# Splitting the output maps of a perceiver prologue into halves by head and placing each half behind its own batch of maxima

## What is computed

```python
x = layer_norm(image_embeds, ln1_g, ln1_b)
l = layer_norm(latents, ln2_g, ln2_b)
q = l @ Wq
kv = concatenate([x, l], axis=1) @ Wkv
k, v = split(kv, 2, axis=-1)          # 16 heads of 64
w = softmax(einsum('bhqd,bhkd->bhqk', q * scale, k * scale))
out = einsum('bhqk,bhkd->bhqd', w, v) # heads side by side: [16, 64, 1024]
return out @ Wo                       # [16, 64, 128]
```

## Time and profile before

| what | value |
|---|---|
| median of 3 runs | 948.94 us |
| lowest and highest | 947.06 and 949.42 us |
| the profiled execution's own time | 947.89 us |
| its span, first to last instruction | 946.2 us |
| mean granted TensorE clock | 0.994 |
| PE busy | 909.3 us (96%) |
| DVE busy | 798.4 us (84%) |
| ACT busy | 701.2 us (74%) |
| POOL busy | 378.3 us (40%) |

### The profile page before, as it was taken

One profiled execution on the slowest core, in us unless ns is written; L12 is line 12 of the kernel. 1 busy time (PEld: TensorE's weight loads), 2 busy tenths in 40 slices (PEclk: granted clock), 3 DMA queues, 4 the chain that ended last, 5 costly groups with the idle time before them and its releaser, 6 DMA issues.

```text
span 946.2 us, 20541 instructions
## 1 busy us (share of the span) xinstructions
PE 909.3 (96%) x8268; PEld 490.1 (52%) x8268; DVE 798.4 (84%) x1591; ACT 701.2 (74%) x1003; POOL 378.3 (40%) x378
## 2 busy tenths in 40 slices
PE   8679999999999999999999999999999999999996
PEld 5444445555454545454545454545454545566763
DVE  5979898979797979898989898888888786588987
ACT  4767878787878787878787878787879676755544
POOL 6472133343444343434343444343434231335345
PEclk9999999999999999999999999999999999999999
DMA  6402030303040303030303030303020200000000
GB/s 214 81 14 61 7 89 2 94 1 95 1 94 1 92 5 83 13 75 21 74 23 73 23 72 24 74 23 73 23 61 23 38 23 2 23 25 24 2 2 23
DMA packets 74566, 41.96 MB, mean 44 GB/s; under 512 B 62276, under 2 KB 69864, under 8 KB 74472
## 3 DMA queue, kind: packets, MB, share of 16 engines
q1 hardware_dynamic: 74184, 39.60, 16.8%
q10 hardware_dynamic: 288, 1.05, 0.3%
HBM read 25.98 MB, written 0.59 MB: 28 GB/s over the span
## 4 chain that ended last, share of the span: by engine, by line
PE 80%; DVE 14%; ACT 3%; issue 2%; DMA 1%; POOL 1%; POOLq 0%; DVEq 0%; ACTq 0%
PE S L2151 10%; PE S L2142 9%; PE OA L2175 9%; PE OA L2178 9%; PE OA L2181 9%; PE S L2145 9%; PE WW L2085 9%; PE WW L2112 1%; PE WW L2113 1%; DVE amx L803 1%; PE WW L2114 1%; PE WW L2072 1%; PE WW L2073 1%; PE WW L2074 1%; DVE mx L1510 1%
## 5 line engine op out<-in xcount | busy, mean ns | idle before, releaser
L1859 ACT ACTIVATE region<-S,sigma 128x1024 f16<-128x1024 f32 x208 | 231.6, 1113 | 135.9 <-PE S L2151 135.9
L1539 DVE TENSOR_TENSOR region<-S,region 128x1024 f16<-128x1024 f32 x208 | 252.4, 1214 | 42.3 <-ACT S L1863 42.3
L1527 DVE TENSOR_REDUCE mx<-WW 128x1 f32<-128x512 f32 (+1 forms) x480 | 262.7, 583 | 29.7 <-PE WW L2085 22.5
L1863 ACT ACTIVATE S<-S,sigma 128x1024 f32<-128x1024 f32 x208 | 224.4, 1079 | 0.0
L1671 POOL TENSOR_TENSOR xk<-raw,xk 128x508 f16<-128x508 f32 x64 | 63.2, 998 | 167.8 <-DVE xk L1406 167.8
L2142 PE MATMUL S<-region,xT 128*128 128x512 f16 (+1 forms) x416 | 124.5, 380 | 3.3 <-DVE region L1539 2.6
L2085 PE MATMUL WW<-xT,region 128*128 128x512 f16 x360 | 124.7, 380 | 3.0 <-DVE region L1518 2.1
L2175 PE MATMUL OA<-region,xk 128*128 128x512 f16 (+1 forms) x416 | 123.8, 379 | 0.0
L2145 PE MATMUL S<-region,xT 128*128 128x512 f16 (+1 forms) x416 | 123.7, 379 | 0.0
L2151 PE MATMUL S<-region,xT 128*128 128x512 f16 (+1 forms) x416 | 123.7, 379 | 0.0
L2178 PE MATMUL OA<-region,xk 128*128 128x512 f16 (+1 forms) x416 | 123.7, 379 | 0.0
(11 more groups left out here) (318 smaller groups left out, 1830.2 us busy)
## 6 DMA issues: line engine op xcount, KB each, us to landing
raw<-ctx SPq DMA_DIRECT2D x16, 768.0 KB
rb<-inv_dram SPq DMA_DIRECT2D x16, 512.0 KB, 3.5
xT<-xk SPq DMA_TRANSPOSE x48, 3.1
left_row<-left_pT SPq DMA_DIRECT2D x48, 2.0 KB
raw<-ctx SPq DMA_DIRECT2D x16, 32.5 KB
WO_lo<-L_xattn_Wq ACTq DMA_DIRECT2D x1, 512.0 KB, 3.8
WO_hi<-L_xattn_Wkv ACTq DMA_DIRECT2D x1, 512.0 KB, 4.7
lx<-x SPq DMA_DIRECT2D x1, 512.0 KB, 5.7
```

The lines of the kernel that those rows point to most:

```text
L1527: nc.vector.tensor_reduce(mx[:, r, c:c + 1], W[BANK[("m", n)]][:, 0:width], AX.X, ALU.max)\
L1539: nc.vector.tensor_tensor(p_lo[k], src, p_hi[k], ALU.subtract).then_inc(lo_done.sem, 1)
L1859: nc.scalar.activation(p_hi[k], src, ACT.Exp, scale=sigma[:, 0:1])
L1863: nc.scalar.activation(src, src, ACT.Exp, scale=sigma[:, 0:1]).then_inc(e_done.sem, 1)
```

## The change

Each pair of output maps is made in two calls, j = 0 (the first head of both groups, four products) and j = 1 (the second head of both). The waits for the evictions of the pair before stay in the first call, and `wo_mapped` is announced by the second. Pair 1 goes behind n = 5 and 6, pair 2 behind n = 7 and 8, pair 3 behind n = 10 and 11. Pair 0 stays whole. No other engine's program changes.

```diff
-            def output_maps(i):
+            def output_maps(i, j):
 
                 for g in (2 * i, 2 * i + 1):
-                    if i > 0:
+                    if i > 0 and j == 0:
                         pe.wait_ge(wo_evicted.sem, g - 1)
-                for j in range(2):
-                    for c in (0, 128):
-                        for g in (2 * i, 2 * i + 1):
-                            h = wo_heads(g)[j]
-                            r = slice(64 * (h % 2), 64 * (h % 2) + 64)
-                            ins = mm(OA[:, g % 2, 256 * j + c:256 * j + c + 128], wvT[r, h // 2, c:c + 128],
-                                     wo_sb[r, h // 2, :], start=True, stop=True)
-                ins.then_inc(wo_mapped.sem, 1)
+                for c in (0, 128):
+                    for g in (2 * i, 2 * i + 1):
+                        h = wo_heads(g)[j]
+                        r = slice(64 * (h % 2), 64 * (h % 2) + 64)
+                        ins = mm(OA[:, g % 2, 256 * j + c:256 * j + c + 128], wvT[r, h // 2, c:c + 128],
+                                 wo_sb[r, h // 2, :], start=True, stop=True)
+                if j == 1:
+                    ins.then_inc(wo_mapped.sem, 1)
+
+            MAPS_BEHIND = {5: (1, 0), 6: (1, 1), 7: (2, 0), 8: (2, 1), 10: (3, 0), 11: (3, 1)}
...
-            output_maps(0)
+            output_maps(0, 0)
+            output_maps(0, 1)
             for n in range(5, 2 * 8):
                 first_maxima(n)
-                if n in (5, 8, 11):
-                    output_maps(n // 3)
+                if n in MAPS_BEHIND:
+                    output_maps(*MAPS_BEHIND[n])
```

## The result

The changed kernel is slower. Its median is 953.01 us over 11 runs (950.81 to 953.97), against 949.33 for the kernel before, measured beside it in 11 runs (947.06 to 952.33). The ratio is 1.0031, with a 95% interval of 1.0018 to 1.0043, so about 2.9 us by the ratio. The forecast was 949.4.

A forecast was written before the change was run, and what follows sets the result against it. It took the prologue's chain through DVE's maxima to `m16` to decide slot 0's start, with PE carrying 80% of the chain. The mean of known executions, 948.33, plus 1.04 for the new wait at low clock gave 949.4 us, range 947.0 to 951.1.

The forecast's parts named there:

- Where the time is decided: Prologue: the change acts only by moving slot 0's start, through DVE's maxima ending in `m16` at 61.27; any delay passes on whole.
- The eviction wait: Behind block 7, half (2,0) waits for pair 1's evictions until 52.30, so block 8 is late; price +0.03 to +1.04 by clock.
- +0.03: Sum of the delay at block 12 in the prologue if the clock stays at 2.4 GHz throughout.
- The clock: Prologue: PE at 1.2 GHz from 51.0 to 54.4 as before the change, making the delay +1.04; chance 0.50.
- An early fall (+0.9): Prologue: the clock falls earlier, around 47.6 to 51, giving a delay of +0.9, inside the bounds.
- a late return (+1.6): Prologue: the low clock is kept to 57.8, so block 11 is reduced by 59.75, a delay of +1.6.
- The bound of +1.6: Upper bound on the prologue's delay, with the low clock kept to 57.8; the lower bound was +0.03.
- The case of a long low stretch: Rival, prologue: the clock stays low long, +1.6, giving 949.9 us; chance 0.12.
- The rivals' line that half (1,1) "gives PE more to do just ahead of 51": Argument for the rival that the prologue's clock holds at 2.4 GHz: 0.0, 948.3 us, chance 0.28.
- The rule: Skill's rule that PE bursts between waits pay the low clock repeatedly; for the prologue it meant +1.6 and not +1.04.
- The second fall in slot 0: Rival: low clock at slot 0's start slows the first six score matmuls by 1.3; +2.9 with the +1.6, 951.2 us; chance 0.05.
- The slower side: Whole kernel slower by over 0.3%, expected only through another clock fall where slot 0 begins; chance 0.05.

The follow-up runs named there:

- second profile of the changed kernel: The changed kernel run again with no edit, profiled in its slowest of nine executions (954.97 us); median 952.59 us, ratio 1.0036 against the kernel before.
- the filled kernel: Changed kernel plus 18 unread products behind half (1,0) and 10 behind block 7, in PE's idle time; median 948.41 us, ratio 0.9985 against the kernel before.
- the two filled kernels: Changed kernel with 18 and 10 unread products (948.41 us, ratio 0.9985), and kernel before with 16 behind pair 1 (947.44 us, ratio 0.9973).
- the kernel filled twice: Kernel before plus 16 unread products behind pair 1 and 28 where PE waits for DVE ahead of 29 us; median 946.48 us, ratio 0.9972.
- only the first idle time filled: Changed kernel plus 18 unread products behind half (1,0) only, none behind block 7; median 948.18 us, ratio 0.9994 against the kernel before.

## Why the prediction was wrong

*Where the time is decided.* Right. The end moved with `m16`: from `m16` to the end of the span it is 946.2 - 61.27 = 884.93 before and 949.0 - 63.82 = 885.18 after. In the second profile of the changed kernel it is 953.2 - 66.21 = 886.99, so there the end moved by 1.8 more than `m16`.

*The eviction wait.* Right in place, and nearly in size: PE was forecast to idle from 50.94 to 52.30 behind block 7, 1.36, and idled 1.15, or 1.48 where the clock was up. Group 3's eviction was forecast to end at 52.15 and ended at 52.30 + 0.68 = 52.98, later because (1,1) ran at 1.2 GHz; block 8 is queued behind PE's wait, and DVE idles before blocks 8 and 11. At 2.4 GHz the forecast sum was +0.03 against the kernel before as profiled, and the filled kernel shows 0.63. (The +0.03 hid two sums, by the filled kernels: 2.11 for the order, less 1.48 that the kernel before lost to the clock.) Of the missing 0.60 the halves give 0.42. A half's hold on PE was taken as 1.10/2 = 0.55, and from start to next start it is 53.43 - 52.79 = 0.64 there, twice on the path. From a half's start over ACT's two evictions to the next pair, 0.64 + 1.93 + 0.15 = 2.72 was taken, and it is 52.79 - 49.95 = 2.84, twice as well. A narrow block ahead of a half holds PE for 53.81 - 53.43 = 0.38 and not for 0.30, which gives 0.16 more. Halving a block of matmuls doesn't halve its time. At 1.2 GHz it is 54.28 - 53.12 = 1.16 and not 1.00.

*The clock.* This is the step that failed. "Clock at 1.2 GHz from 51.0 to 54.4, as before" took the place and the length of the low stretch over from the trace of before, though the change alters the very activity that it hangs on. An early fall (+0.9) and a late return (+1.6) were both worked out, but as alternatives. In the changed kernel both happened together: low from 47.4 to 57.7, +2.69 in the fastest execution, and low from 49.5 to 63.1, 17.18 - 12.87 = +4.3, in the slowest of the nine repeats. With the level kept up by unread products the same order takes 13.50, so of the 15.56 the low stretch makes 2.06. The bound of +1.6 was no bound. The case of a long low stretch stood among the rivals with a chance of 0.12, but it was priced for a late return alone.

*What the trace of before showed and I passed over.* With (1,1) gone, PE's idle time ahead of block 6 had to grow from 1.90 by the half's 0.55; it measured 2.34. The 1.27 stands before it, with only 0.71 of work between. I counted the eviction moving later and not what the stretch lost. The rivals' line that half (1,1) "gives PE more to do just ahead of 51" looked at where the work went and not where it came from.

*The rule.* It was weighed on "one fall" in the prologue, but rows 6 begin at 34.00. The same view of the kernel before has a second low stretch just ahead of them, from 30.5 to 34.0:

```profile
30.40:34.00 3.60, 3.60 (x31) 2.61 (x29) 3.37 (x4) 3.01 (x4) 0.50 (x2) 0.53 1.01 104
```

The Trainium skill (TensorE: Matmul & The Clock Gate, "HAM oscillation — how this bites in real kernels") says that bursts between waits keep paying; the waits in its case are for DMA and longer, about 3 to 5 us, than PE's 2.34 and 1.15 in the changed kernel. The profile sides with the rule on direction: with both new idle times the level stays low over several blocks. It doesn't on form: the level didn't go up and down with the bursts, it stayed down through them.

*The second fall in slot 0.* Not seen in the two profiles; the clock was up by 63.1 at the latest. The slower side came about through the case beside it.

*What stays open.* The medians of the two filled kernels differ by 948.41 - 947.44 = 0.97 while their profiles' distances differ by 13.50 - 11.39 = 2.11. Both can be right: the two spans, 946.7 and 945.8, differ by 0.9 as well, since from `m16` to the end it takes 946.7 - 62.20 = 884.5 in the one and 945.8 - 60.12 = 885.7 in the other, and the extra lies in single slots (last section). Whether a slot takes longer because `m16` came earlier isn't shown, so it is open how much of the order's 2.11 reaches the end in general. And why the level stays low for 10.2 us in one execution and for 13.7 in another isn't shown by any row; in both PE was busy for over 70% of the stretch.

## What to carry to other kernels

Where a row shows a low clock, don't carry its place and length over to the changed kernel, nor from one execution to the next: list which idle times of PE the change lengthens, and bound the cost by the low level over the whole neighbourhood, early fall and late return at once. Work that stands in a gap in which PE waits anyway is free there, and as the fillings show it can keep the clock up; moved behind a wait it costs its own time and delays its neighbours. And when a half is put in front of a wait for another engine, check that as many blocks lie between a pair and the wait for its eviction as the eviction takes.

## What the runs showed that was not expected

Matmuls whose results nobody reads made the kernel faster: 16 in one idle time of PE gave 0.27%, and the eight runs agree within 0.64 us where those of the kernel before, beside them, spread from 947.1 to 952.0. A part of that kernel's scatter goes with the clock: the six of these runs above 951 are the ones with the lowest mean granted clock, 0.988. It isn't all of it: of the ten runs of the kernel filled twice, the nine with a clock of 0.997 or 0.998 still spread from 944.95 to 947.07.

Another part lies in the slots. Apart from the first and the last, `m16` of each slot follows the one before by 47.88 us. In eleven of the twelve profiles single distances are up to 1.6 longer. Where no unread products were added it is the fourth distance in all seven profiles (48.53 before, 48.86 and 49.40 in the two of the changed kernel); where they were, it is another or, with only the first idle time filled, none. In the second profile of the changed kernel:

```profile
158.59 0.19 DVE L1532 TENSOR_REDUCE m<-mx 128x8 f16<-128x32 f32 x1
...
206.47 0.19 DVE L1532 TENSOR_REDUCE m<-mx 128x8 f16<-128x32 f32 x1
...
255.87 0.19 DVE L1532 TENSOR_REDUCE m<-mx 128x8 f16<-128x32 f32 x1
...
303.91 0.19 DVE L1532 TENSOR_REDUCE m<-mx 128x8 f16<-128x32 f32 x1
```

That is 47.88, 49.40 and 48.04. The clock reads 1.00 there, and the cause is open.
